# A two-layer recurrence on one core: three waits move, and one bias write of ScalarE moves one step earlier

## What is computed

```python
def layer(x, h0, Wx, Wh, b):
    xW = einsum('ntd,dh->nth', x, Wx) + b
    def step(h_prev, xw_t):
        h_next = tanh(h_prev @ Wh + xw_t)
        return (h_next, h_next)
    ...
x = x + layer(x, cond_1024, L0_cond_Wx, L0_cond_Wh, L0_cond_b)
x = x + layer(x, cond_1024, L1_cond_Wx, L1_cond_Wh, L1_cond_b)
```

## Time and profile before

| what | value |
|---|---|
| median of 3 runs | 2145.44 us (2143.24 to 2146.1) |
| profiled execution, its own time | 2143.24 us |
| span of the profiled execution | 2141.5 us |
| mean granted TensorE clock | 0.998 |
| busy: TensorE matmul / weight load | 2112.9 us (99%) / 1960.2 us (92%) |
| busy: VectorE / ScalarE | 1761.9 us (82%) / 1121.1 us (52%) |

### The profile page before, as it was taken

The page is one execution under the profiler, slowest core; times in us unless marked ns, Lnnn a source line. Parts: engine busy times, 40 slices in busy tenths (PEclk is TensorE's granted clock), DMA queues, the critical chain, the costliest instruction groups (busy, mean ns, idle before and its releaser), DMA issues.

```text
span 2141.5 us, 205681 instructions
## 1 busy us (share of the span) xinstructions
PE 2112.9 (99%) x94368; PEld 1960.2 (92%) x94368; DVE 1761.9 (82%) x10233; ACT 1121.1 (52%) x4609; POOL 11.7 (1%) x15
## 2 busy tenths in 40 slices
PE   7999999999999999999999999999999999999997
PEld 6899999999999999999999999999999999999996
DVE  4788888888888888888888888888888888888886
ACT  3455555555555555555555555555555555555553
POOL 2000000000000000000000000000000000000000
PEclk9999999999999999999999999999999999999999
DMA  3000000000000000000000000000000000000000
GB/s 102 23 26 23 26 23 25 24 25 25 24 26 23 26 23 26 23 26 23 26 24 25 25 24 25 24 26 23 26 23 26 23 26 23 26 24 25 25 24 16
DMA packets 112074, 56.18 MB, mean 26 GB/s; under 512 B 12448, under 2 KB 111024, under 8 KB 111536
## 3 DMA queue, kind: packets, MB, share of 16 engines
q1 hardware_dynamic: 111456, 53.53, 8.7%
q10 hardware_dynamic: 432, 1.18, 0.2%
q0 software_dynamic: 32, 0.02, 0.0%
HBM read 37.90 MB, written 16.78 MB: 26 GB/s over the span
## 4 chain that ended last, share of the span: by engine, by line
PE 98%; DMA 1%; issue 0%; DVE 0%; ACT 0%; SPq 0%; ACTq 0%
PE ps_rec L225 53%; PE ps_rec L238 24%; PE ps_xw L206 21%; DMA wx<-wx_in 0%; DMA x_pe<-x_t 0%; DVE zt L370 0%; DVE z L376 0%; ACT h L305 0%; SPq L177 0%; SPq L175 0%; ACT ps_rec L300 0%; ACT ps_xw L293 0%; DVE x_out L420 0%; DVE h L384 0%; ACTq L304 0%
## 5 line engine op out<-in xcount | busy, mean ns | idle before, releaser
L225 PE MATMUL ps_rec<-wh,h 128*32 128x128 f32 x41024 | 1484.9, 273 | 16.3 <-ACT h L305 12.0
L225 PEld LDWEIGHTS ps_rec<-wh,h 128*32 128x32 f32 x41024 | 1089.4, 109 | 69.6 <-ACT h L305 18.3
L305 ACT ACTIVATE h<-z 128x32 f32<-128x32 f32 x2048 | 470.5, 230 | 869.5 <-DVE z L376 853.3
L238 PE MATMUL ps_rec<-wh_part,h 128*32 128x128 bf16 x36768 | 881.1, 220 | 2.9 <-issue 2.8
L384 DVE TENSOR_TENSOR h<-h 128x8 f32<-128x8 f32 (+1 forms) x4080 | 611.1, 150 | 302.8 <-ACT h L305 302.4
L300 ACT ACTIVATE ps_rec<-ps_xw,mask 128x128 f32<-128x128 f32 x2048 | 670.6, 328 | 135.4 <-PE ps_xw L206 109.7
L238 PEld LDWEIGHTS ps_rec<-wh_part,h 128*32 128x32 bf16 x36768 | 631.3, 97 | 100.3 <-issue 4.1
L370 DVE STREAM_TRANSPOSE zt<-ps_rec 128x128 f32<-128x128 f32 x2048 | 648.3, 317 | 32.9 <-PE ps_rec L225 16.4
L376 DVE TENSOR_REDUCE z<-zt 128x32 f32<-128x96 f32 x2048 | 544.2, 266 | 1.5 <-DVE zt L370 0.9
L206 PE MATMUL ps_xw<-wx,x_pe 128*32 128x128 f32 x8192 | 403.9, 273 | 4.0 <-DMA wx<-wx_in 2.5
L206 PE MATMUL ps_xw<-wx,x_mid 128*32 128x128 f32 x8192 | 402.0, 273 | 1.2 <-issue 1.2
(11 more groups left out here) (14 smaller groups left out, 12.6 us busy)
## 6 DMA issues: line engine op xcount, KB each, us to landing
x_pe<-x_t SPq DMA_DIRECT2D x256, 64.0 KB, 1.9
x_dve<-x_t SPq DMA_DIRECT2D x256, 64.0 KB, 2.0
out_t<-x_out SPq DMA_DIRECT2D x256, 64.0 KB, 1.5
wx<-wx_in SPq DMA_DIRECT2D x4, 256.0 KB, 7.8
wh<-wh_in ACTq DMA_DIRECT2D x1, 1024.0 KB, 8.3
wh<-wh_in SPq DMA_DIRECT2D x1, 1024.0 KB, 6.3
wx<-wx_in SPq DMA_DIRECT2D x1, 1024.0 KB, 8.3
bias<-b_in ACTq DMA_DIRECT2D x2, 64.0 KB, 3.1
```

What stands on the lines that cost most here:

```text
L225: mm = pe.matmul(rows(bank, g), h_step(l, n - 1)[:, k, :], wh[l][:, k, g * P:(g + 1) * P], start=False, stop=k == KC - 1 and whole.start = ...
L238: mm = pe.matmul(rows(bank, g), h_bits(l, n - 1)[:, k, :], wh_part[l][:, i, at:at + P], start=False, stop=k == whole.start - 1 and i == PA ...
L305: act.activation(h_of(l, n), z[l][n % 2][:, :].rearrange("p (k b) -> p k b", k=KC), ACT.Tanh).then_inc(h_last if (l, n) == (0, T - 1) else ...
```

## The change

On ScalarE, the wait for x_pe moves from behind `tanh(0, 4k+1)` to ahead of `tanh(0, 4k+2)`. The wait for x_mid (`mid_done`) moves from behind `tanh(0, 4k)`, where `begin(0, 4k+2)` follows, to ahead of `tanh(1, 4k-8)` of the same slot. `seed(1, c)` moves from the end of slot 4c+3 to the end of slot 4c+2. On VectorE, the wait for x_dve moves from the head of `sums` in slot 4c to ahead of `sum_mid(4c)`, which is issued in slot 4c+1. No arithmetic changes, and TensorE's and SyncE's programs stay as they are.

```diff
             def tanh(l, n):
+                c = n // S4 + 1 if l else (n + 6) // S4
+                if l == 0 and n % S4 == 2 and 2 <= c < NG:
+                    act.wait_ge(x_pe_loaded[c % 2], DMA * (c // 2))
+                if l == 1 and n % S4 == 0 and c < NG:
+                    act.wait_ge(mid_done, c + 1)
                 act.wait_ge(z_done[l], n + 1)
...
-                    if l == 0 and s % S4 == 1 and 2 <= (c := (s + 7) // S4) < NG:
-                        act.wait_ge(x_pe_loaded[c % 2], DMA * (c // 2))
-                    if l == 0 and s % S4 == 0 and 2 <= (c := s // S4) <= NG:
-                        act.wait_ge(mid_done, c)
...
-                    if l == 1 and s % S4 == 3 and 2 <= (c := s // S4) < NG:
+                    if l == 1 and s % S4 == 2 and 2 <= (c := s // S4) < NG:
                         act.wait_ge(begun[1], S4 * (c - 1))
                         seed(1, c)
...
             def sum_mid(n):
                 c, t = n // S4, n % S4
+                if t == 0:
+                    dve.wait_ge(x_dve_loaded[c % 2], DMA * (c // 2 + 1))
...
             def sums(s):
-                c = (s + S4 - 1) // S4
-                if s % S4 == 0 and c < NG:
-                    dve.wait_ge(x_dve_loaded[c % 2], DMA * (c // 2 + 1))
```

## The result

The changed kernel takes 2162.4 us (median of 6 runs, 2160.74 to 2164.52), the kernel before, run beside it, 2143.85 us (6 runs). The ratio is 1.0086, 95% interval 1.0074 to 1.0099. That is slower by 18.5 us where 6.8 was forecast, and outside the range.

The account below looks back on a forecast made before the run. One layer's closed ring of 2.04 us, through TensorE, VectorE and ScalarE's tanh, was taken to set the slot. Seed +7.0 and start -0.2 gave +6.8 us, on 2145.44 making 2152.2 us; range 2146 to 2159.

Parts of the forecast that it names:

- The ring is closed: Layer 0's round from weight load through matmuls, transpose, reduction and tanh to the next load: 2.04 us, setting the slot.
- The rival that the page's chain named: TensorE is the real bound, leaving only the start's gain, 2145.2 us; one case of the swallowed delay, chance 0.21 together.
- the load's constant 0.05: On TensorE, the weight load starts 0.05 us behind its layer's tanh wherever looked, except at loop ends.
- The moved seed: On ScalarE, the tanh of slot 4k+3 ends 0.055 us later in 127 places, +7.0 us.
- I take 0: On VectorE, the second wait at `sum_mid`, for x_dve, becomes an instruction of its own and costs 0.
- costs nothing either: On ScalarE, the moved wait for x_mid finds x_mid long ready ahead of layer 1's tanh: no cost, no gain.
- The wait on VectorE: Rival: x_dve's separate wait adds a 0.03 hand-over 254 times, 7.6 us more, 2159.8; within slower cases, chance 0.12 together.
- The start's -0.2 us: At the start, moving x_pe's wait takes the seed out of the way; the tanh comes 0.2 us earlier, once.
- Loop ends: At the end of TensorE's loop, 0.09 us of layer 0's and 0.05 of layer 1's tanh delay is free; costed nothing.
- a gap of 0.085: At loop ends, the forecast time from the late tanh's end to layer 0's weight load, 0.14 - 0.055 us.

Follow-up runs that it names:

- thin_proj: The kernel before with the projection's matmuls over 64 of 128 columns in all four column groups; 2109.41 us, ratio 0.9836.
- thin_xpe: thin_proj with the wait for x_pe also moved ahead of the tanh of slot 4k+2; 2125.01 us, ratio 0.9907 to the kernel before.
- dve_only: The kernel before with only the wait for x_dve moved from the head of `sums` to the head of `sum_mid`; 2144.48 us, ratio 1.0004.
- seed_only: The kernel before with only the seed of layer 1 moved one slot earlier; 2144.37 us, ratio 1.0003.
- waits_all: The changed kernel with the seed back in its old slot, so only the three waits moved; 2159.64 us, ratio 1.0069 to the kernel before.
- swap_noseed: waits_all with the late wait written first where two stand ahead of one instruction; 2142.83 us, ratio 0.9994 to the kernel before.
- swap_all: The changed kernel with the late wait written first where two stand ahead of one instruction; 2145.48 us, ratio 1.0004 to the kernel before.

## Why the prediction was wrong, step by step

- *"The ring is closed: its length is 2.04 us [...] and nothing in it is idle but hand-overs."* This step failed. The hand-over from tanh to weight load was read rightly, but the ring also holds the way from the load to its matmul, and 0.04 of that was waiting in line. I took the timeline rows as a closed account without looking whether the matmul starts when its load does. The rival that the page's chain named, TensorE as the bound, was right: 98% was no artefact. It was dismissed with the load's constant 0.05, which shows that the load waits for the tanh, not that the matmul does. thin_proj and thin_xpe showed it. The rule of the Trainium skill, "Perfetto Trace Analysis" (section on the most contended engine), that the share of weight loads tells more than matmul busy time, didn't help here: with 92% of weight loads TensorE was the pace all the same.
- *The moved seed.* Order and spacings came as forecast (0.26 and 0.20 for 0.27 and 0.205). Its price, 127 x 0.055 = 7.0, was 0.8 by itself (interval -1.3 to +2.6): the delay of 0.05 is about as large as the room.
- *"It is taken while `sum_out` ahead of it still runs. I take 0"*, and likewise for x_pe and x_mid: "costs nothing either". This step failed and made the time. I asked whether the awaited thing was there, which it was, but not which of two waits the separate instruction would carry. In the written order it carried the late one, and its 0.07 stands behind the reduction, where no idle time covers it. With 254 places for x_pe and 255 for x_mid: 254 x (0.07 - 0.045) = 6.4 for one wait, where 8.0 and 6.3 were measured.
- *The wait on VectorE.* I had this one as a rival at 7.6 us. It did show, 0.29 instead of 0.21, but cost 0.9, not to be told from nothing: VectorE had made it up to 0.01 by the transpose (dve_only).
- *The start's -0.2 us.* The tanh came at 19.55 with the one before it at 17.35, so 2.20 instead of 19.46 - 17.16 = 2.30 (the earlier one from the same view of the kernel before): half of it, and far below what a run can tell.
- *Loop ends.* No price by a short delay, as forecast: in seed_only the weight load at 1007.35 is 0.09 behind the end of the late tanh (1007.04 + 0.22), where a gap of 0.085 was forecast.
- *The account.* 8.0 + 6.3 + 0.9 = 15.2 for the waits, as waits_all measured, and 0.8 for the seed make 16.0 of 18.5 us. The remaining 2.5 is open. The intervals reach some 2 to 3 us to either side each, so it may be nothing. The seed's tanh comes one slot behind the late tanh of x_pe, which may leave it less room: between waits_all and the changed kernel the seed is worth about 3 us. But between swap_noseed and swap_all, where no tanh ahead of it is late, it is worth 2.7 as well, so this reason isn't shown.

That the sign came out as forecast is luck: the reason given for it was worth about 1 of 18.5 us.

## What to carry to other kernels

Where two waits stand ahead of one instruction, ask which becomes an instruction of its own, and write them so that the late one stays with the instruction; here the late one written last cost 0.07 us a time, and written first nothing that could be told. Before a dependency is called the pace, follow it to the first instruction that does the work (the matmul, not its weight load) and look whether that one stands in line. If two limits lie within 2%, as 2.04 and 2.00 here, a single delay shorter than the distance is nearly free, but a longer or a constant one is paid.

## What of the hardware was unexpected

- A wait as an instruction of its own on ScalarE took 0.02, with 0.04 more until the next instruction started. With the first hand-over of 0.02 the tanh started 0.08 behind the reduction, with a single wait 0.03, both read from chains.
- Matmuls in four column groups run as four streams: leaving out two groups left the slot at 2.04 (only 11 us in all came off), while halving the columns in all four took off 34.7 us.
